# Three GpSimd folds and one narrow product of ones for the routed weights' column norms, placed behind the unit's down product

## The reference, cut to what matters

```python
x = x + attention(layernorm(x), w_qkv, w_out, decay_param)       # 16 heads, decayed running sums
h = layernorm(x)
scores = softmax(h @ gate_w)                                     # 8 experts
topk_w, topk_idx = top_k(scores, 2)
routed = sum over the token's 2 experts e of topk_w * (silu(h @ w_gate[e]) * (h @ w_up[e])) @ w_down[e]   # 512 x 352 x 512
shared = (silu(h @ sw_gate) * (h @ sw_up)) @ sw_down             # 512 x 704 x 512
out = x + routed + shared
```

## Time and profile before

| | |
|---|---|
| time, three runs | 739.93 us median (736.96 to 740.67) |
| profiled execution, its own time | 738.84 us |
| its span | 736.8 us |
| PE busy | 655.2 us, 89% of the span |
| DVE busy | 441.9 us, 60% |
| ACT busy | 235.7 us, 32% |
| POOL busy | 215.4 us, 29% |
| mean granted TensorE clock | 0.977 |
| chain that ended last | DMA 33%, PE 31%, DVE 16%, issue 12% of the span |

### The profile page before, as it was taken

How to read it: one execution, slowest core, us unless ns; L and a number is a source line. 1 busy time by engine, 2 the same in 40 slices (tenths; PEclk the granted TensorE clock), 3 DMA queues, 4 the chain that set the end, 5 groups by cost and what they waited for, 6 DMA issues and landing times.

```text
span 736.8 us, 11499 instructions
## 1 busy us (share of the span) xinstructions
PE 655.2 (89%) x3677; PEld 422.1 (57%) x3678; DVE 441.9 (60%) x808; ACT 235.7 (32%) x353; POOL 215.4 (29%) x234
## 2 busy tenths in 40 slices
PE   3979889879899599899998999999899899989982
PEld 2757567558577365465655656655455555545551
DVE  6879888987997661786876976433322232232221
ACT  4343421242342212446665664411111111111110
POOL 6100111101102026333432333143344433334431
PEclk9999999999999799899999999999999999999998
DMA  6840003512433577975855316367666666676662
GB/s 215 280 127 16 15 19 83 161 39 58 117 84 86 132 170 205 273 179 149 183 150 147 58 29 79 66 114 129 128 118 121 120 120 123 125 128 118 118 96 39
DMA packets 111235, 86.87 MB, mean 118 GB/s; under 512 B 79280, under 2 KB 86448, under 8 KB 111200
## 3 DMA queue, kind: packets, MB, share of 16 engines
q1 hardware_dynamic: 88848, 43.94, 25.0%
q0 software_dynamic: 12272, 27.34, 20.8%
q10 hardware_dynamic: 10080, 15.14, 6.8%
HBM read 44.45 MB, written 23.33 MB: 92 GB/s over the span
## 4 chain that ended last, share of the span: by engine, by line
DMA 33%; PE 31%; DVE 16%; issue 12%; ACT 2%; POOL 2%; SPq 2%; POOLq 1%; DVEq 0%; ACTq 0%
DMA out_dram<-y_job,job_tok 26%; PE ring L378 12%; PE ps_y L504 5%; PE ps_g L504 5%; PE ps_u L504 5%; DMA shared<-in_L_attn_w_out_dram 2%; DVE run_kv L1205 1%; DMA routed<-in_L_ffn_w_down_dram 1%; DVE routed L1347 1%; DVE run_kv L1197 1%; SPq L771 1%; PE turn_h L524 1%; DVE run_k L1193 1%; DVE xn L1167 1%; DMA x_in<-in_L_attn_x_dram 1%
## 5 line engine op out<-in xcount | busy, mean ns | idle before, releaser
L1287 DVE TENSOR_TENSOR hidT<-turn_h,hidT 128x384 f16<-128x384 f32 x71 | 39.5, 556 | 129.4 <-ACT hidT L1036 129.2
L911 POOL DMA_INDIRECT out_dram<-y_job,job_tok x39 | 61.4, 1574 | 142.1 <-DVE y_job L1638 74.8
L504 PE MATMUL ps_g<-routed,x_in 128*128 x468 | 76.5, 313 | 17.1 <-DMA x_in<-x_job 17.0
L378 PE MATMUL ring<-xnT_h,wq_h 128*128 128x512 f32 x192 | 81.1, 422 | 11.3 <-DVE run_kv L1197 4.2
L1032 ACT ACTIVATE silu<-ps_g,job_silu 128x352 f32<-128x352 f32 x39 | 21.6, 553 | 209.1 <-PE ps_g L504 209.1
L504 PE MATMUL ps_y<-routed,hidT 128*128 x351 | 82.1, 379 | 1.3 <-DVE hidT L1287 1.3
L378 PE MATMUL ring<-xnT_l,wq_h 128*128 128x512 f32 x192 | 78.1, 407 | 0.0
L378 PE MATMUL ring<-xnT_h,wq_l 128*128 128x512 f32 x192 | 77.9, 406 | 0.0
L836 POOL TENSOR_SCALAR var_eps<-mean_var 128x1 f32<-128x1 f32 x32 | 11.7, 367 | 226.4 <-DVE mean_var L1268 125.7
L504 PE MATMUL ps_u<-routed,x_in 128*128 x468 | 76.2, 313 | 0.0
L504 PE MATMUL ps_y<-shared,hidT 128*128 128x512 f16 x288 | 69.3, 387 | 7.5 <-DVE hidT L1287 7.4
(11 more groups left out here) (222 smaller groups left out, 1062.9 us busy)
## 6 DMA issues: line engine op xcount, KB each, us to landing
routed<-in_L_ffn_w_gate_dram ACTq DMA_DIRECT2D x7, 704.0 KB, 4.8
routed<-in_L_ffn_w_up_dram ACTq DMA_DIRECT2D x7, 704.0 KB, 9.0
x_res<-in_L_attn_x_dram SPq DMA_DIRECT2D x18, 256.0 KB, 3.2
out_dram<-x SPq DMA_DIRECT2D x16, 256.0 KB, 3.3
xn_scratch<-xn_hl SPq DMA_DIRECT2D x16, 256.0 KB, 2.5
out_dram<-y_job POOLq DMA_DIRECT2D x16, 256.0 KB, 4.2
x_in<-in_L_attn_x_dram SPq DMA_DIRECT2D x14, 256.0 KB, 2.7
routed<-in_L_ffn_w_down_dram ACTq DMA_DIRECT2D x7, 512.0 KB, 10.8
```

The costliest lines, as they stand in the source:

```text
L378: ins = pe.matmul(ps, a, b, start=(i == 0), stop=(i == len(steps) - 1))
L504: ins = pe.matmul(ps, a[i][:, k, :], w(j, k), start=(start and q == 0), stop=(stop and q == len(steps) - 1))
L911: pool.indirect_dma_start(out[:, :], bass.IndirectOffsetOnAxis(job_tok[:, r:r + 1], 0), y_job[:, b, :], None, compute_op=ALU.add).then_inc ...
L1287: dve.tensor_tensor(hidT[:, 1], turn_h[:, 0:FC, :], hidT[:, 0], ALU.subtract).then_inc(s["hidT_s"], 1)
```

## The change

A routed piece is folded three times by GpSimd, so that an eighth of the width is left (176 or 192 columns), each fold waiting for the one before by a new semaphore `narrow_s`; the last sets `fold_s`. TensorE makes one product of ones over that width in place of two over a quarter each. The call of `column_norms` moves from ahead of the ranking, table and down products to behind the down product of the same unit. The maximum on DVE reads 176 or 192 columns in place of 352 or 384: sums of column pairs, still a bound on each column's norm. Shared pieces (six, during the attention) stay as they are. DVE's and ACT's order is unchanged.

```diff
         def norms_of(m):
-            n = pieces[m][3].shape[1] // 4
-            return ps_gate[:, P:P + n] if m < SHARED_PIECES else ps_norm[:, 0:n]
+            n = pieces[m][3].shape[1]
+            return ps_gate[:, P:P + n // 4] if m < SHARED_PIECES else ps_norm[:, 0:n >> ROUTED_FOLDS]
...
                 pe.wait_ge(s["fold_s"], m + 1)
                 if m:
                     pe.wait_ge(s["max_s"], m)
-                n = w.shape[1] // 4
-                for k in range(2):
+                parts = 2 if m < SHARED_PIECES else 1
+                n = norms_of(m).shape[1]
+                for k in range(parts):
                     ins = pe.matmul(norms_of(m), ones_h[:, :], squares[:, k * n:(k + 1) * n],
-                                    start=(k == 0), stop=(k == 1))
+                                    start=(k == 0), stop=(k == parts - 1))
                 ins.then_inc(s["norm_mm"], 1)
...
-                if norm_unit(u - 1) is not None:
-                    column_norms(norm_unit(u - 1))
                 if u == RANK_UNIT:
                     rank_tokens()
                 for m in table_choices(u - 1):
                     table_product(m, start=m == 0, stop=m == TOPK * NT - 1)
                 down_product(u, t, shared_down(half), half == 0, half == 1, t == 0)
+                if norm_unit(u - 1) is not None:
+                    column_norms(norm_unit(u - 1))
...
                 half = pieces[m][3].shape[1] // 2
                 pool.wait_ge(s["square_s"], m + 1)
-                pool.tensor_tensor(squares[:, 0:half], squares[:, 0:half], squares[:, half:2 * half], ALU.add)\
-                    .then_inc(s["fold_s"], 1)
+                for i in range(ROUTED_FOLDS):
+                    if i:
+                        pool.wait_ge(s["narrow_s"], (m - SHARED_PIECES) * (ROUTED_FOLDS - 1) + i)
+                    pool.tensor_tensor(squares[:, 0:half], squares[:, 0:half], squares[:, half:2 * half], ALU.add)\
+                        .then_inc(s["narrow_s" if i < ROUTED_FOLDS - 1 else "fold_s"], 1)
+                    half //= 2
```

More of the change, by code:

```diff
@@ L248, in preln_decay_attention_moe @@
             gw_h_s gw_l_s gate_mm logit_s x2_out0 x2_out1 xn2_out0 xn2_out1 pad_out cst_a cst_b shared_in
-            over_0 w0 w1 w2 w3 w4 w5 w6 w7 square_s fold_s norm_mm max_s set_s upper_s split_s
+            over_0 narrow_s w0 w1 w2 w3 w4 w5 w6 w7 square_s fold_s norm_mm max_s set_s upper_s split_s
             d_set d_route rt_exp rt_exp_in picked_s hot_s route_mm tables_s xin0 xin1 gin0
@@ L293, in split_pieces @@
             return [SHARED_PIECES + 3 * e + i for e in range(E) for i in range(3) if split_unit(e) + i == u]
+        ROUTED_FOLDS = 3
         def norms_of(m):
-            n = pieces[m][3].shape[1] // 4
-            return ps_gate[:, P:P + n] if m < SHARED_PIECES else ps_norm[:, 0:n]
+            n = pieces[m][3].shape[1]
+            return ps_gate[:, P:P + n // 4] if m < SHARED_PIECES else ps_norm[:, 0:n >> ROUTED_FOLDS]
         FREE_PARTS = 2 * KC
```

## The result

The changed kernel takes 759.31 us (median of 4, 758.13 to 760.43) against 738.71 us for the kernel before, measured beside it: ratio 1.0271, interval 1.0233 to 1.0308. The direction was forecast; the size was not, 20.6 us instead of 10.3, and 759.3 lies above the range. One of the twelve executions of experiment 10 took 1112.52 us at a mean granted clock of 0.563 and has no part in its ratio.

The account below looks back on a forecast made before the run. TensorE was taken as the bound, DVE not far behind. From 738.84 us, minus 5.5 for shorter products, plus 13.0 for late DVE chains, plus 2.9 for added folds, came 749.2; range 741 to 757.

Parts of the forecast that it names:

- TensorE's gain: One narrow product of ones for two in 24 routed pieces: 5.5 us saved; a unit with tables lasts 6.03 us.
- The chains behind the maximum: DVE's later maximum delays the rest half of the hidden in heavy units, so down products wait: 13.0 us lost.
- rival 3: TensorE's clock falls in waits of units 20 and 25, 2 to 2.5 us a fall: 751 to 754; chance 0.15.
- The folds: GpSimd's later folds: hidden in plain units, blocking DVE in nine units at 0.3 us each, 2.9 us lost.
- The first fold blocks as before: First GpSimd fold still meets DVE's scale steps; up to 1.3 us of this is already in the chain lengths.
- rival 5: Each of the three folds blocks DVE in the nine heavy units: full 7.2 us, 753.5; chance 0.14.
- Against it: the waits of units 5 to 25 left the clock at 1.00: The argument against rival 3: the kernel before kept full granted clock through its waits in that stretch.
- The list of units with work behind the maximum: Units whose DVE chain was priced: 5, 6, 7, 10, 13, 16, 18, 19, 21, 24, 27; together 13.0 us.
- 749.2: Forecast time in us for the profiled execution, stated as 749; chance 0.48.
- hidden in plain units by their late start: In plain units DVE's split goes first and GpSimd's folds end at 5.3 us, before the product at 5.95: no cost.

Follow-up runs that it names:

- experiment 10: experiment 6 with two folds, one product over a quarter, and TensorE's waits for the last splits moved to the products that read them; 739.17 us, ratio 1.0013.
- experiment 2: Kernel before, with only the call moved: one fold and two products of ones, behind the down product; 757.03 us, ratio 1.0252.
- experiment 6: Changed kernel, with DVE's maximum one unit later, behind the next unit's hidden, and splits of experts 4 to 7 one unit later; 740.06 us, ratio 1.0010.
- experiment 8: experiment 6 with two folds and one product of ones over a quarter; 743.03 us, ratio 1.0070.
- experiment 3: Changed kernel, with filler products of ones on TensorE ahead of the down product in the units that waited; 753.54 us, ratio 1.0200.
- experiment 1: Changed kernel without the move: three folds and one narrow product of ones, ahead of the down product; 747.52 us, ratio 1.0115.
- experiment 9: experiment 6 with TensorE's waits for the last splits moved to the products that read them; 735.36 us, ratio 0.9967.
- experiment 5: experiment 1 with two folds and one product of ones over a quarter, ahead of the down product; 743.96 us, ratio 1.0058.

## Why the prediction was half right

**TensorE's gain, 5.5 us.** Right in its parts: 0.08 us from the product of ones to the next gate product, 6.04 us for a free unit against the stated 6.03.

**The chains behind the maximum.** Right. The waits forecast for single down products, against those measured: units 6 to 8 1.3 each against 2.0, 1.4 and 1.1; units 11, 17 and 19 1.3 to 1.6 against 2.07, 2.07 and 2.02; units 14 and 22 1.7 against 2.06 and 2.12; unit 20, for which rival 3 has about 3.4, against 2.96; unit 25 3.35 against 3.66; unit 28 0.5 against 0.60. Experiments 2 and 6 show the mechanism from both sides: the move alone makes it, and a place further back on DVE's queue takes it away. In the sum, 13.0 and 2.9 for the folds, 15.9, stand against a measured 16.8.

**The folds.** The first fold blocks as before, as stated. Folds of 352 and 176 columns are a little longer than the stated 0.80 and 0.45: 0.85 (shortest, experiment 8) and 0.52. For the others I took 0.3 us in each of nine units. The rows of unit 10 show one more block of 0.67 (2.49 against 1.82) by the second fold and none by the third, which itself waits; experiment 2 puts the added folds at 4.6 us of waits. The rule from the Trainium skill (SBUF — State Buffer, Who interferes with whom), that the operation issued first holds the ports to its end, fits each of these rows; what it can't say is which comes first, and here DVE's split beat the third fold. The full 7.2 us of rival 5 was too much.

**What failed, first: "Against it: the waits of units 5 to 25 left the clock at 1.00".** The waits of the kernel before in that stretch were up to 1.7 us. I carried this over to waits of 2 us and more, and the sum has no term for the clock at all; even the two waits of over 3 us counted only in rival 3. Measured were six falls, one of them with a wait of 2.65, three with waits of 2.02 to 2.12 and two with the waits of units 20 and 25 that rival 3 names, for 9.4 us. Experiment 3 shows the cause for four of the six, 6.5 of the 9.4 us; units 5 and 25 are read from the timeline alone. Rival 3 had the mechanism, at 2 to 2.5 us for each of two falls; measured are 1.3 to 1.7 us for each of six, down and gate product together, since the lower level held for 3.4 us and about half of that is lost.

**Second: unit 5.** The list of units with work behind the maximum left out unit 4, whose step finds the best experts and sets `picked`. TensorE's ranking products of unit 5 wait for that ahead of the down product. The chain started 3.7 us later against the next gate product than before, the first fold held one of its casts for 1.50 us, and TensorE waited 2.65 us, with a fall of the clock behind it: 2.7 and 1.3 us.

749.2 with 12.1 for these two is 761.3. The forecast was made for a profiled execution, and that of the changed kernel took 760.43.

**Not foreseen in the parts:** I had the added folds hidden in plain units by their late start. That is right for the moved product, but ahead of the down product they are not hidden at all (experiment 1), so neither half of the change gains anything, alone or with the other.

## What to carry to other kernels

When a producer is moved later on the engine that is the bound, look at the consumer's queue on the other engine: all that stands behind the consumer moves too, and the wait comes back through the next thing the bound engine needs. Moving the consumer behind that thing, one step later, gave back 19 of 20.6 us here, though not the 5.5 us that the shorter products should have brought. And a wait of some 2 us of TensorE is to be priced with the chance that its clock falls with it, 1.3 to 1.7 us each time here, and 9.4 us in all.

## What the runs showed that I had not expected

- The clock doesn't fall with every wait. Of the waits of 2.0 to 2.2 us of the down product in the changed kernel and in experiments 1, 6, 8, 9 and 10 (six, one and twelve), ten came with a slow down product (3, 0 and 7), the others not, in otherwise equal units; the 2.10 us of experiment 3, with filler ahead of it, came with one too. Beyond unit 4 those of up to 1.9 us never did, and the seven of 2.62 us and more, in the changed kernel and in experiments 1, 2 and 5, always. What decides between equal waits stays open.
- When it falls isn't tied to the work's new start. Read from windows of 0.25 us, it fell in unit 20 of the changed kernel 0.1 us ahead of it, in units 5 and 6 0.1 us after it, in units 11 and 22 0.8 and 1.0 after, and in unit 25 1.35 after; at unit 4 of the kernel before it fell in the wait, 1.9 us ahead of the down product. In all six cases of the changed kernel the lower level held for 3.4 us. So each of these six cost about the same wherever it came: 1.6 or 1.7 us, and 1.3 in unit 5. Two that came over a microsecond ahead of the work's new start, at unit 4 of the kernel before and in unit 20 of experiment 1, held for 6.8 us. The rows are units 20 and 25 of the changed kernel, then unit 4 of the kernel before:

```profile
417.00:419.45 2.45, 0.00 (x0) 0.00 (x0) 1.48 (x2) 2.45 (x5) 1.74 (x1) 1.00 0.48 107
419.45:422.90 3.45, 3.28 (x8) 1.20 (x9) 2.65 (x5) 0.89 (x1) 2.54 (x3) 0.51 0.13 12
...
459.10:460.45 1.35, 1.35 (x7) 0.64 (x8) 0.43 (x1) 0.00 (x0) 0.00 (x0) 1.00 0.00 0
460.45:463.85 3.40, 3.40 (x13) 1.59 (x12) 1.83 (x2) 1.83 (x2) 0.38 (x1) 0.50 0.02 5
...
296.65:303.40 6.75, 4.89 (x13) 1.94 (x14) 5.68 (x51) 1.13 (x3) 1.20 (x3) 0.50 1.02 297
```

- A chain of three folds by GpSimd on 704 columns takes mostly 3.0 to 3.4 us where it is free and 4.4 where a split comes between (340.57 in experiment 6, 349.25 above): the third fold, 0.52 us at its shortest, had a mean of 1.05 in the changed kernel (176 columns, first row).

```profile
L925 POOL TENSOR_TENSOR squares<-squares 128x176 bf16<-128x176 bf16 x16 | 16.9, 1054 | 1.3
L925 POOL TENSOR_TENSOR squares<-squares 128x352 bf16<-128x352 bf16 x16 | 14.2, 890 | 1.3
```
